# Two slots at a time in the first expert layer of a two-layer transformer kernel

## The reference, cut to what matters

```python
# B*T = 4096 rows x_ of C = 128 features, E = 8 experts, H = 256 hidden columns
idx = jnp.argmax(x_ @ router.T, axis=-1)              # one expert for each token
u = jnp.einsum('bc,ehc->ebh', x_, up)
g = jnp.einsum('bc,ehc->ebh', x_, gate)
ye = jnp.einsum('ebh,ech->ebc', jax.nn.silu(g) * u, down)
y = jnp.einsum('ebc,be->bc', ye, onehot(idx))         # only the chosen expert counts
ys = jax.nn.silu(x_ @ w_gate_s.T) * (x_ @ w_up_s.T) @ w_down_s.T    # shared expert
return y + ys
```

## Time and profile before

| | before |
|---|---|
| median of 3 runs | 1011.62 us (1010.07 to 1012.82) |
| profiled execution, first to last instruction (its span) | 1020.2 us |
| its own time beside that span | not given apart from the span |
| PE busy | 939.7 us, 92% |
| DVE / ACT / POOL busy | 62% / 54% / 45% |
| first layer's slot loop in the profile | about 557 to 629 us |

### The profile page before, as it was taken

One profiled execution on the slowest core, in us unless ns is written; L12 is line 12 of the kernel. 1 busy time (PEld: TensorE's weight loads), 2 busy tenths in 40 slices (PEclk: granted clock), 3 DMA queues, 4 the chain that ended last, 5 costly groups with the idle time before them and its releaser, 6 DMA issues.

```text
span 1020.2 us, 21591 instructions
## 1 busy us (share of the span) xinstructions
PE 939.7 (92%) x7416; PEld 604.4 (59%) x7416; DVE 633.1 (62%) x2087; ACT 554.9 (54%) x1078; POOL 462.6 (45%) x698
## 2 busy tenths in 40 slices
PE   8999999999989989999994898889997999999996
PEld 3566777777654233334642886456664644499994
DVE  4789998999815966853642444567773653344444
ACT  6536767667657555565421554558775522255551
POOL 1146776777642946620064554344552044323331
PEclk9999999999999989999997999999999999999999
DMA  6700000000020000040012225100000010111115
GB/s 208 229 2 3 3 2 2 3 2 2 3 83 11 0 1 1 0 165 0 1 48 63 73 76 167 31 2 2 2 2 1 1 32 29 48 44 50 49 32 175
DMA packets 32601, 42.01 MB, mean 41 GB/s; under 512 B 6960, under 2 KB 26800, under 8 KB 31632
## 3 DMA queue, kind: packets, MB, share of 16 engines
q1 hardware_dynamic: 27952, 31.26, 9.8%
q0 software_dynamic: 4544, 9.38, 2.8%
HBM read 29.16 MB, written 16.66 MB: 45 GB/s over the span
## 4 chain that ended last, share of the span: by engine, by line
PE 71%; issue 14%; ACT 6%; DVE 5%; DMA 2%; POOL 1%; SPq 1%; DVEq 0%; POOLq 0%; ACTq 0%
PE PS L693 6%; PE PS L434 5%; PE PS L676 5%; PE PS L476 5%; PE PS L683 5%; PE PS L447 4%; PE PS L330 3%; PE PS L339 3%; PE PS L627 3%; PE PS L629 3%; PE PS L636 2%; PE PS L536 2%; PE PS L427 2%; PE PS L783 2%; PE PS L802 2%
## 5 line engine op out<-in xcount | busy, mean ns | idle before, releaser
L911 ACT ACTIVATE pw<-PS 128x384 f32<-128x384 f32 x256 | 111.6, 488 | 71.5 <-PE PS L456 68.9
L1588 POOL TENSOR_SCALAR_AFFINE_SELECT pw<-pw 128x256 f32<-128x256 f32 x256 | 105.1, 434 | 75.0 <-ACT pw L911 73.1
L1186 DVE CUSTOM_DVE_ANT_0 PS<-PS,above 128x256 f32<-128x256 f32 x256 | 115.9, 453 | 23.0 <-PE PS L427 22.8
L1654 POOL DMA_INDIRECT token_rows<-xnb,slot_in x78 | 75.0, 962 | 119.3 <-ACT xnb L1014 113.5
L1640 POOL TENSOR_TENSOR XS<-XS,N 128x512 f32<-128x512 f32 x64 | 81.2, 1292 | 55.2 <-DVE N L1264 34.6
L434 PE MATMUL PS<-kf,qm 32*128 32x256 f32 x512 | 103.6, 426 | 0.5 <-POOL qm L1597 0.5
L1440 DVE TENSOR_TENSOR rsb<-sqb,PS 128x256 f32<-128x256 f32 (+1 forms) x78 | 43.2, 554 | 95.8 <-PE PS L683 44.1
L1188 DVE CUSTOM_DVE_ANT_0 PS<-PS,above 128x128 f32<-128x128 f32 x256 | 84.7, 331 | 0.0
L1610 POOL TENSOR_SCALAR_AFFINE_SELECT pw<-pw 128x256 f32<-128x256 f32 x128 | 56.1, 472 | 60.7 <-ACT pw L1059 60.7
L1597 POOL TENSOR_SCALAR qm<-qs,qmask 128x256 f32<-128x256 f32 x64 | 59.7, 933 | 44.1 <-ACT kf L892 44.1
L997 ACT ACTIVATE sqb<-PS 128x512 f32<-128x512 f32 x48 | 28.7, 597 | 88.9 <-PE PS L627 81.0
(11 more groups left out here) (214 smaller groups left out, 2406.6 us busy)
## 6 DMA issues: line engine op xcount, KB each, us to landing
sorted_rows<-empty_rows_dram SPq DMA_DIRECT2D x2, 2535.0 KB, 14.6
slot_in<-sorted_rows SPq DMA_DIRECT2D x78, 65.0 KB
N<-token_rows SPq DMA_DIRECT2D x16, 256.0 KB, 4.7
X<-xT_dram SPq DMA_DIRECT2D x8, 256.0 KB, 5.7
ATT<-gate_dram SPq DMA_DIRECT2D x1, 2048.0 KB
XS<-down_dram SPq DMA_DIRECT2D x1, 2048.0 KB
H<-up_dram SPq DMA_DIRECT2D x1, 2048.0 KB
out_dram<-X SPq DMA_DIRECT2D x8, 256.0 KB, 3.8
```

The costliest lines, as they stand in the source:

```text
L911: nc.scalar.activation(pw[:, w % 2, j + n, :], PS[:, A_PST + (2 * v + n) % 3, 0:3 * P], ACT.Exp).then_inc(a_p, 1)
L1186: nc.vector.tensor_tensor_reduce(x[:, 0:SEQ], x[:, 0:SEQ], above[:, :], 1.0, -3e38, ALU.add, ALU.max, mx[:, t // 8 % 2, 1, j, g:g + 1])
L1588: m = nc.gpsimd.affine_select(x[:, :, SEQ * k:SEQ * k + P], x[:, :, SEQ * k:SEQ * k + P], [[0, 2], [1, P]], ALU.is_ge, 0.0, base=0, channe ...
L1654: nc.gpsimd.indirect_dma_start(token_rows[l][:, :], bass.IndirectOffsetOnAxis(slot_in[:, r, D:D + 1].bitcast(mybir.dt.int32), 0), slot_out ...
```

## The change

In the first layer, slots are worked in groups of two (GROUP = (2, 1): two in the first layer, one in the second); the last group has one slot. A group g has the PSUM bank that a slot had, so its two slots fill 512 columns instead of 256: one Silu, one product and one copy of the turned rows serve both slots. The semaphores `xk`, `xf`, `gate`, `up`, `wgate`, `wup`, `silu`, `hidden` and `down` count groups; `y` still counts slots. The number of matmuls, weight copies, register loads, weightings, loads and sends stays. On PE the register loads move from before `turn` to behind `sum_down`, and stand two in a row. The loop's lead of two slots becomes two groups: `turn(0)` and `turn(1)` now turn four slots before the first `gate_up`.

```diff
+        GROUP = (2, 1)
+        GROUPS = [-(-SLOTS // g) for g in GROUP]
+        def group(l, g):
+            return range(g * GROUP[l], min((g + 1) * GROUP[l], SLOTS))
+        def of_group(l, g):
+            return l * GROUPS[0] + g + 1
...
-                        sp.wait_ge(q["xk"], l * SLOTS + k - RING + 1)
+                        sp.wait_ge(q["xk"], of_group(l, (k - RING) // GROUP[l]))
...
+                def turn(g):
+                    if g:
+                        pe.wait_ge(q["xf"], of_group(l, g - 1))
+                    for i, k in enumerate(group(l, g)):
+                        pe.wait_ge(q["load"][k % RING], of_slot(l, k))
+                        m = nc.tensor.transpose(PS[:, 7, i * P:(i + 1) * P], slot_in[:, k % RING, 0:D], ident[:, :])
+                    m.then_inc(q["xk"], 1)
...
+                    for i in range(slots):
+                        for n in range(i * HID, (i + 1) * HID, P):
+                            m = nc.tensor.matmul(PS[:, b, n:n + P], wgate[:, b, n:n + P], xnb[:, b, i * P:(i + 1) * P],
+                                                 start=True, stop=True)
...
+                    pe.wait_ge(q["hidden"], of_group(l, g))
+                    if g:
+                        pe.wait_ge(q["y"], l * SLOTS + g * GROUP[l])
...
-                    if k + 1 < SLOTS:
-                        columns[k + 1] = first_column(k + 1)
-                    if k + 2 < SLOTS:
-                        turn(k + 2)
-                    if k:
-                        sum_down(k - 1, columns[k - 1])
+                    if g + 2 < GROUPS[l]:
+                        turn(g + 2)
+                    if g:
+                        sum_down(g - 1)
+                    if g + 1 < GROUPS[l]:
+                        columns.update({k: first_column(k) for k in group(l, g + 1)})
...
+                    nc.scalar.activation(sqb[:, b, 0:w], PS[:, b, 0:w], ACT.Silu).then_inc(q["silu"], 1)
+                def weight(g):
+                    act.wait_ge(q["down"], of_group(l, g))
+                    for i, k in enumerate(group(l, g)):
...
+                    nc.vector.tensor_tensor(rsb[:, b, 0:w], sqb[:, b, 0:w], PS[:, 2 + b, 0:w],
...
+                    nc.vector.tensor_copy(xnb[:, g % 2, 0:w], PS[:, 7, 0:w]).then_inc(q["xf"], 1)
```

More of the change, by code:

```diff
@@ new lines, in gate_up @@
+                def gate_up(g):
+                    b, slots = g % 2, len(group(l, g))
+                    pe.wait_ge(q["xf"], of_group(l, g))
+                    pe.wait_ge(q["wgate"], of_group(l, g))
+                    if g >= 2:
+                        pe.wait_ge(q["silu"], of_group(l, g - 2))
+                    for i in range(slots):
+                        for n in range(i * HID, (i + 1) * HID, P):
+                            m = nc.tensor.matmul(PS[:, b, n:n + P], wgate[:, b, n:n + P], xnb[:, b, i * P:(i + 1) * P],
+                                                 start=True, stop=True)
+                    m.then_inc(q["gate"], 1)
+                    pe.wait_ge(q["wup"], of_group(l, g))
+                    if g >= 2:
+                        pe.wait_ge(q["hidden"], of_group(l, g - 2))
+                    for i in range(slots):
+                        for n in range(i * HID, (i + 1) * HID, P):
+                            m = nc.tensor.matmul(PS[:, 2 + b, n:n + P], wup[:, b, n:n + P], xnb[:, b, i * P:(i + 1) * P],
+                                                 start=True, stop=True)
+                    m.then_inc(q["up"], 1)
@@ new lines, in sum_down @@
+                def sum_down(g):
+                    b = g % 2
+                    pe.wait_ge(q["hidden"], of_group(l, g))
+                    if g:
+                        pe.wait_ge(q["y"], l * SLOTS + g * GROUP[l])
+                    for i, k in enumerate(group(l, g)):
+                        for n in range(NH):
+                            m = nc.tensor.matmul(PS[:, 6, i * D:(i + 1) * D], rsb[:, b, i * HID + n * P:i * HID + (n + 1) * P],
+                                                 down_f[:, bass.ds(columns[k] + n * D, D)], start=(n == 0), stop=(n == NH - 1))
@@ L1000, in moe, with silu @@
                     shared_silu(j)
[L1002 to L1015, removed]
+                def silu(g):
+                    b, w = g % 2, len(group(l, g)) * HID
+                    act.wait_ge(q["gate"], of_group(l, g))
+                    if g >= 2:
+                        act.wait_ge(q["hidden"], of_group(l, g - 2))
+                    nc.scalar.activation(sqb[:, b, 0:w], PS[:, b, 0:w], ACT.Silu).then_inc(q["silu"], 1)
+                def weight(g):
+                    act.wait_ge(q["down"], of_group(l, g))
+                    for i, k in enumerate(group(l, g)):
+                        if k >= OUTS:
+                            act.wait_ge(q["sent"][(k - OUTS) % RING], of_slot(l, k - OUTS))
+                        nc.scalar.activation(slot_out[:, k % OUTS, :], PS[:, 6, i * D:(i + 1) * D], ACT.Copy,
+                                             scale=slot_in[:, k % RING, D + 1:D + 2]).then_inc(q["y"], 1)
                 gate_f = c["gate"].rearrange("p e h -> p (e h)")
@@ L1020, in first_column, with fetch_gate @@
                     return act.value_load(eid[0:1, k:k + 1], min_val=0, max_val=c["cap"] * HID)
-                def fetch_gate(k, e):
-                    nc.scalar.activation(wgate[:, k % 2, 0:HID], gate_f[:, bass.ds(e, HID)], ACT.Copy).then_inc(q["wgate"], 1)
-                act.wait_ge(q["eid"], l + 1)
[L1027 to L1038, removed]
+                def fetch_gate(g):
+                    for i, k in enumerate(group(l, g)):
+                        m = nc.scalar.activation(wgate[:, g % 2, i * HID:(i + 1) * HID], gate_f[:, bass.ds(columns[k], HID)],
+                                                 ACT.Copy)
+                    m.then_inc(q["wgate"], 1)
+                act.wait_ge(q["eid"], l + 1)
+                columns = {k: first_column(k) for g in range(3) for k in group(l, g)}
+                fetch_gate(0)
+                fetch_gate(1)
+                for g in range(GROUPS[l] + 1):
+                    if g < GROUPS[l]:
+                        silu(g)
+                    if g + 2 < GROUPS[l]:
+                        fetch_gate(g + 2)
+                    if g + 3 < GROUPS[l]:
+                        columns.update({k: first_column(k) for k in group(l, g + 3)})
+                    if g:
+                        weight(g - 1)
                 for j in range(NCH * NH - LATE, NCH * NH):
@@ L1451, in first_column, with fetch_up @@
                     return dve.value_load(eid[0:1, k:k + 1], min_val=0, max_val=c["cap"] * HID)
[L1453 to L1455 removed]
+                def fetch_up(g):
+                    for i, k in enumerate(group(l, g)):
+                        m = nc.vector.tensor_copy(wup[:, g % 2, i * HID:(i + 1) * HID], up_f[:, bass.ds(columns[k], HID)])
+                    m.then_inc(q["wup"], 1)
                 dve.wait_ge(q["eid"], l + 1)
[L1458 to L1460 removed]
+                columns = {k: first_column(k) for g in range(3) for k in group(l, g)}
+                fetch_up(0)
+                fetch_up(1)
                 copy_x(0)
                 copy_x(1)
[L1463 to L1469, removed]
+                for g in range(GROUPS[l]):
+                    gate_hidden(g)
+                    if g + 2 < GROUPS[l]:
+                        copy_x(g + 2)
+                        fetch_up(g + 2)
+                    if g + 3 < GROUPS[l]:
+                        columns.update({k: first_column(k) for k in group(l, g + 3)})
                 shared_next(LATE)
```

48 lines of the change are left out of this document (13 added, 35 removed).

## The result

| | before | after |
|---|---|---|
| median of 20 runs each, us | 1012.9 (1010.1 to 1017.7) | 1017.61 (1013.0 to 1019.9) |
| ratio | 1 | 1.0046 [1.0031, 1.0061] |
| profiled execution: span, own time | 1020.2, not shown | 1016.9, 1018.71 |

The change costs 0.0046 x 1012.9 = 4.7 us. That is outside the range of 1001.5 to 1016, on the side to which I gave 0.19.

A forecast was written before the change was run, and what follows sets the result against it. The prediction took TensorE (PE), busy 939.7 of 1020.2 us, as the bound. Gain 0, start 1.0 and end 1.2 sum to +2.2 us; 1011.62 + 2.2 = 1013.8 us, range 1001.5 to 1016.

The forecast's parts named there:

- Register loads on PE: Two loads in a row behind `sum_down`: 1.3 us without new work, covered by 2.0 us of queued work, 0 us.
- rival D: First loop: the pair of register loads starves PE, 20 groups x 0.3 = 6 us, total 1019.8 us; chance 0.10.
- Holes not in the timed runs: First slot loop: PE's 11.6 us of holes are the profiler's and absent from timed runs; chance 0.46.
- gain of 0: First slot loop: gain from closing PE's holes, bounds 11.6 us and 0, taken as 0.
- So the change covers the holes wherever they exist: First loop: slack for late results grows from 0.4 to 1.5 us, more than the 1.17 of lateness.
- slack of 1.5 us: First loop after the change: copied rows are ready at 2.3 us, transposes due at 3.8, leaving 1.5 us.
- Rival C: First loop: timed runs have some holes, or late signals outlast the slack; with half, 1008.0 us; chance 0.17.
- Product, Silu and copy of double width, 0 us: First loop: one of each for two slots, 0.688, 0.597 and 0.416 us, on engines about half busy, costs nothing.
- Start, +1.0: First loop's start: the first gate matmuls come 1.4 us later, 0.44 was done later before; cost 1.0 us.
- end, +1.2: First loop's end: the last three sends stand in a row and PE waits for the rows; cost 1.2 us.
- Ring, 0: SP's waits by groups hold a load back by at most one slot in twelve, 1.45 us against 17; 0 us.

The follow-up runs named there:

- both_ends2: The change with single slots at the loop's start and end, pairs between, register loads still behind `sum_down`: 1017.64 us, 1.0056 of before.
- singles4: The changed kernel with groups of one slot, leaving only the register load moved behind `sum_down`: 1017.18 us, 1.0053 of before.
- ring10: The change with 10 places of slot_in instead of 12, in both layers: 1031.57 us, 1.0184 of before.
- late set: A set of runs, compared only within itself, in which the kernel before ran at 1022 to 1024 us.
- prompt set: A set of runs, compared only within itself, in which the kernel before ran at 1012 to 1013 us.
- after_third: The changed kernel repeated without alteration, where before took 1022.83 us: 1024.30 us, 1.0006 of before.
- before_again: The kernel before, unchanged, profiled once more in one execution: 1021.24 us, beside a median of before of 1021.68.
- regs_early: The change with pairs kept and PE's register loads put back ahead of `turn`, where before took 1021.68 us: 1025.74 us, 1.0030.
- regs_early2: The same kernel as regs_early, measured where before took 1013.25 us: 1013.76 us, 1.0006 of before.
- before_timed: The kernel before, unchanged, timed and profiled as an experiment of its own: 1011.00 us, 0.9991 of before.
- after_again: The changed kernel repeated without alteration, timed and profiled beside before: 1019.35 us, 1.0062 of before.
- set 2: The runs of after_again and before_timed with their own runs of before, whose median was 1012.16 us.

## Why the prediction was wrong, point by point

- **The step that failed** is *Register loads on PE*: "2.0 us of work in the queue. So 1.3 is covered, 0 us." Measured, that term is 4 to 6 us and not 0: 0.46 to 0.62% with the loads behind `sum_down` (change twice, both_ends2, singles4), 0.06 and 0.08% with them ahead of `turn` or gone. The 2.0 us came from the second loop, whose `gate_up` is 16 passes and not 8, and from a kernel whose load stands behind `gate_up`. Behind `sum_down` in the first loop what is issued ahead is 0.89 us for a pair, 0.445 for one slot, and the loads start late when a wait of `turn` or `sum_down` ahead of them ends late. The prediction also had "1.0 us" of the first loop, in rival D, and set it aside for the second loop's.
- **Rival D** (0.10) named the mechanism and a size, 20 x 0.3 = 6 us, that is close to what was measured; its 1019.8 contains start and end on top. The size is in part luck: its 1.0 us is the lead of one slot behind `gate_up`, a place where no load stands after the change. And it is not the pair. One load at that place costs as much, since two slots' down passes cover two loads no better than one slot's cover one: 0.89 for 1.4 us against 0.445 for 0.6.
- **Holes not in the timed runs: right for these runs, for a wrong reason.** I laid them to profiling ("so profiling lengthens this kernel by 8.6 us"). In every set the profiled execution's own time is 1.7 to 2.0 us over its span and, except for ring10, among the timed runs beside it. With 1.7 to 2.0 added, the profile ahead of the prediction is at about 1022 us, a late set's time, and the median beside it is a prompt set's; that the two came from executions of different kinds is inferred from this, since the profile's own time is not on record. The gain of 0 that I took was so the right term, by luck: the result was measured in a prompt set. The Trainium skill ("Runtime: NRT & Kernel Launch", the section on the preamble and postamble), which I had weighed, has a profile's total 6.2 us longer than the reported time; no run here shows that.
- **"So the change covers the holes wherever they exist": wrong.** In the late set after_third has as many passes as before_again. Whether it is the slack of 1.5 us that is too short there was not isolated. The same kernel in a late set (regs_early, 305 passes) and in a prompt one (regs_early2, 361), waits from 562 to 618 us:

```profile
DVE rsb L1458 <- ACT sqb L1022: 12.4, 4, 4.4
```
```profile
DVE rsb L1458 <- ACT sqb L1022: 2.6, 2, 1.5
```

  The longest wait of a product for its Silu is 2.9 us longer in the late one, more than the 1.17 that I had taken as the lateness. Rival C had this in half a sentence ("the late signals outlast the slack").
- **Product, Silu and copy of double width, 0 us: right in a prompt set.** regs_early2 has 361 passes and 1.0006. The sizes were as taken, 0.688 and 0.597. The rule of the Trainium skill ("Perfetto Trace Analysis", the section on optimizing Scalar and DVE operations), that breaking such instructions up may help where they cause bubbles, found nothing to mend in the prompt sets.
- **Start, +1.0, and end, +1.2: not confirmed.** First load issue to first gate matmul is 559.29 - 556.30 = 2.99 in before_timed and 560.63 - 556.78 = 3.85 in after_again: 0.86 and not 1.4, less 0.44 for the two transposes done later before, 0.4. The last down matmuls to the last send are 619.01 - 617.62 = 1.39 and 625.66 - 622.90 = 2.76: 1.4, as foreseen. But from the last down matmuls to the first row turned back it is 625.54 - 617.62 = 7.92 and 630.81 - 622.90 = 7.91: the first rows came back sooner behind the last send, 5.15 us against 6.53, so the end's cost does not reach PE's next work in these profiles. From the first load's issue to the first row turned back, before_timed takes 625.54 - 556.30 = 69.2, regs_early2 627.40 - 555.97 = 71.4, after_again 630.81 - 556.78 = 74.0 and singles4 630.23 - 554.93 = 75.3 us. The pairs with early loads are 2.2 over before, the number of the two terms but not the thing: in that profile the granted clock stayed at 0.50 (1.2 GHz) to 565.0 us, 5.1 us after the first gate matmul, in before_timed to 562.4, 3.1 after it. At half the pace the 2.0 us more cost half of themselves, by my estimate 1.0 of the 2.2. The loads behind `sum_down` bring the change to 4.8, near its timed cost. The timed regs_early2 has 0.6 [-1.2, 2.4]: 2.2 is inside, and the measurement does not separate start and end from nothing.
- **Ring, 0: right at 12 places with early loads**, and nearer to the edge than the step says. At 10 places it is 12 to 14 us; at 12, rows that come late put off the register loads behind them, as at 598.22 in set 2.

Left open: why some row loads land 3.3 us after their issue and others 1.8; what puts off the pair at 576.49; what makes a set late (not the chip alone: sets 1, 2 and 4 ran on the same one, 1 and 4 late, 2 prompt); and the 0.14 to 0.3% that early loads with pairs cost in late sets. No version tried beat before.

The end's two intervals, before_timed and then after_again:

```profile
617.62 0.71 PE L693 MATMUL PS<-down,rsb 128*128 x4 [0.65 <-ACT xnb L1014]
...
619.01 0.96 POOL L1654 DMA_INDIRECT token_rows<-xnb,slot_in  x1 [0.40 <-ACT xnb L1014]
...
625.54 1.42 PE L723 MATMUL PS<-ident,N 128*128 128x128 f32 x8 [1.45 <-DMA N<-token_rows]
```
```profile
622.90 0.71 PE L708 MATMUL PS<-down,rsb 128*128 x4 [0.90 <-ACT xnb L1029]
...
625.66 0.95 POOL L1675 DMA_INDIRECT token_rows<-xnb,slot_in  x1 [0.30 <-issue]
...
630.81 0.66 PE L738 MATMUL PS<-ident,N 128*128 128x128 f32 x4 [1.80 <-DMA N<-token_rows]
```

## What to carry to other kernels

On an engine that is the bound, put a register load behind the largest block of work that has just been issued, not behind a short block that itself waited; count the lead at the new place, in the changed loop. Test a moved instruction alone before the restructuring it came with gets the blame. A releaser named in a profile is to be checked against what the engine's own sequencer did last. And before a difference between a profile and a median is called the profiler's, take both from the same set of runs and compare the profile's own time with them.

## What the runs showed of the hardware

- One kernel can run at two speeds, by sets of runs and on the same chip: in some sets before takes 1022 to 1024 us and PE has 299 passes in the stretch, in others 1012 to 1013 and 361, with the granted clock of the stretch at 1.00 in both. In the slow ones products start up to 1.2 us late behind finished matmuls.
- A gap of 0.1 to 0.2 us on PE does not lower its busy time: 39.98 us of 40 with 322 passes, 40.00 with 361. The count of passes shows it.
- The load of a block of 128 rows landed 1.7 to 2.0 us after its issue in most cases in after_again, and 2.9 to 3.3 us after it in three (issued at 579.0, 592.8 and 605.6).
- A register load costs PE's sequencer 0.6 us from first to last row (584.7 to 585.3), two in a row 1.4 (568.2 to 569.6), against 0.45 of load and register operation alone.
